# Adapter products in quads, with blocks of up, down, down, up between them, in a TensorE-bound FFN kernel

## The reference, cut to what matters

```python
w = weight[adapter_ids]
y = jnp.einsum('bsi,boi->bso', x, w)              # first products, "lora"
t = y.reshape(b * l, Dm)[:, perm].reshape(b * l, h, d)
t = jnp.einsum('bhd,hdm->bhm', t, up)             # "up"
t = jax.nn.gelu(t, approximate=False)
t = jnp.einsum('bhm,hmd->bhd', t, down)           # "down"
x = x + t.reshape(b * l, h * d)[:, argsort(perm)].reshape(b, l, Dm)
```

## Time and profile before

| | before |
|---|---|
| median of 3 runs | 301.78 us (300.81 to 303.13) |
| profiled execution, its own time | 302.47 us |
| its span (first to last instruction) | 300.6 us |
| mean granted TensorE clock | 0.997 |
| PE busy | 293.7 us, 98% of the span |
| DVE busy | 177.6 us, 59% |
| ACT busy | 159.0 us, 53% |
| POOL busy | 98.7 us, 33% |

### The profile page before, as it was taken

How to read it: one execution, slowest core, us unless ns; L and a number is a source line. 1 busy time by engine, 2 the same in 40 slices (tenths; PEclk the granted TensorE clock), 3 DMA queues, 4 the chain that set the end, 5 groups by cost and what they waited for, 6 DMA issues and landing times.

```text
span 300.6 us, 4303 instructions
## 1 busy us (share of the span) xinstructions
PE 293.7 (98%) x1672; PEld 211.3 (70%) x1672; DVE 177.6 (59%) x210; ACT 159.0 (53%) x179; POOL 98.7 (33%) x92
## 2 busy tenths in 40 slices
PE   8999999999999999999999999999999999999994
PEld 3778888888888758586685857858587685544441
DVE  2778769769765963594736847466564723333332
ACT  3637336347439462854429363392824507777750
POOL 3000000188250064181632617130471535222234
PEclk9999999999999999999999999999999999999998
DMA  6999999999996878579675767755376193421335
GB/s 201 324 426 422 420 419 409 317 338 394 393 365 231 340 269 324 177 247 324 221 293 209 277 237 267 271 195 190 120 253 222 70 303 120 136 73 70 139 142 209
DMA packets 23555, 77.87 MB, mean 259 GB/s; under 512 B 2672, under 2 KB 11248, under 8 KB 18544
## 3 DMA queue, kind: packets, MB, share of 16 engines
q1 hardware_dynamic: 6912, 43.39, 39.2%
q0 software_dynamic: 7488, 25.18, 23.4%
q10 hardware_dynamic: 9136, 9.05, 8.8%
HBM read 60.82 MB, written 16.78 MB: 258 GB/s over the span
## 4 chain that ended last, share of the span: by engine, by line
PE 91%; DMA 3%; SPq 2%; issue 1%; DVE 1%; POOL 1%; ACT 0%; POOLq 0%; DVEq 0%
PE ps L535 38%; PE ps L536 19%; PE ps L584 18%; PE ps L563 6%; PE ps L566 5%; PE ps L569 5%; DMA w_raw<-w 3%; SPq L217 1%; POOL out_late L286 1%; SPq L194 1%; DVE w_lo L405 0%; ACT w_hi L317 0%; DVE w_raw L438 0%; SPq L223 0%; POOLq L307 0%
## 5 line engine op out<-in xcount | busy, mean ns | idle before, releaser
L535 PE MATMUL ps<-x_pair,w_hi 128*128 128x512 f32 x480 | 171.0, 401 | 0.7 <-DVE w_lo L405 0.7
L536 PE MATMUL ps<-x_pair,w_lo 128*128 128x256 f32 x480 | 134.7, 281 | 0.0
L535 PEld LDWEIGHTS ps<-x_pair,w_hi 128*128 128x128 f32 x480 | 90.2, 188 | 29.9 <-issue 7.2
L351 ACT ACTIVATE hidden<-ps 128x1024 f32<-128x1024 f32 x64 | 61.0, 1030 | 63.3 <-PE ps L569 56.6
L317 ACT ACTIVATE w_hi<-w_raw 128x1024 fp32r<-128x1024 f32 x60 | 60.4, 1060 | 60.4 <-PE ps L536 32.3
L536 PEld LDWEIGHTS ps<-x_pair,w_lo 128*128 128x128 f32 x480 | 90.6, 189 | 0.0
L405 DVE TENSOR_TENSOR w_lo<-w_raw,w_hi 128x1024 fp32r<-128x1024 f32 x60 | 70.7, 1219 | 13.6 <-ACT w_hi L317 13.6
L259 POOL DMA_INDIRECT t_raw<-y_rows,idx x32 | 33.6, 1049 | 107.7 <-DMA y_rows<-y_out 86.1
L429 DVE TENSOR_REDUCE y_out<-ps 128x256 f32<-128x512 f32 x64 | 42.6, 686 | 41.1 <-PE ps L536 28.5
L584 PE MATMUL ps<-hidden,down_sb 128*64 128x512 f32 x256 | 58.2, 598 | 0.0
L584 PEld LDWEIGHTS ps<-hidden,down_sb 128*64 128x64 f32 x256 | 17.0, 136 | 33.4 <-issue 33.0
(11 more groups left out here) (28 smaller groups left out, 112.5 us busy)
## 6 DMA issues: line engine op xcount, KB each, us to landing
w_raw<-w SPq DMA_DIRECT2D x30, 1024.0 KB
y_rows<-y_out ACTq DMA_DIRECT2D x32, 256.0 KB
x_raw<-x_cols SPq DMA_DIRECT2D x7, 1024.0 KB, 8.0
w_raw<-w SPq DMA_DIRECT2D x4, 256.0 KB, 4.8
hidden<-up SPq DMA_DIRECT2D x1, 1024.0 KB, 10.0
down_sb<-down SPq DMA_DIRECT2D x1, 1024.0 KB, 9.8
w_raw<-w SPq DMA_DIRECT2D x2, 384.0 KB, 7.1
x_raw<-x_cols ACTq DMA_DIRECT2D x2, 256.0 KB, 3.6
```

The lines of the kernel that those rows point to most:

```text
L351: nc.scalar.activation(hidden[:, f % HS, m, :, :], up_banks(f, m)[:, :, :], ACT.Gelu).then_inc(gelu_done, 1)
L535: nc.tensor.matmul(acc, w_hi[:, ws, k, col], x_pair[:, xs, k, :, :], start=(k == 0), stop=False)
L536: last = nc.tensor.matmul(acc[:, 0, :], w_lo[:, ws, k, col], x_hi[:, xs, k, :], start=False, stop=(k == KT - 1))
```

## The change

The lora units go by quads q (one batch each). Behind quad 2 comes up pair 0 alone; behind each of the quads 3 to 6 a block of four pairs, for block k = q - 2: up pair 2k - 1, down pair 2k - 2, down pair 2k - 1, up pair 2k. Nothing stands behind quad 7 but the rest: up pair 9, down pair 8, up pair 10, and so on in turn. The banks and the waits on them follow from the new order, and ACT, DVE and POOL get orders of their own to match. `w_high` of the unit after the next now stands ahead of `y_park` of the same unit, except the one for unit 4q + 5, which stands behind the quad, ahead of the gelus of up pair 2k. Warm-up matmuls write `ps[3]` in place of `ps[0]`.

The core of the diff, PE's order and its waits first:

```diff
-            for j in range(GROUPS):
-                if j > 0:
-                    for g in lora_of(j):
+            for q in range(QUADS):
+                k = block_behind(q)
+                for g in lora_of(q):
+                    if g >= PAIR:
                         lora_unit(g)
-                for f in up_of(j):
+                if k:
+                    for f in units(2 * k - 1):
+                        up_unit(f)
+                    for f in units(2 * k - 2):
+                        down_unit(f)
+                    for f in units(2 * k - 1):
+                        down_unit(f)
+                if k is not None:
+                    for f in units(2 * k):
+                        up_unit(f)
+            for p in range(TURNS, PAIRS):
+                for f in units(p):
                     up_unit(f)
-                for f in down_of(j):
+                for f in units(p - 1):
                     down_unit(f)
+            for f in units(PAIRS - 1):
+                down_unit(f)
```

```diff
 # lora_unit
-                j = g // PAIR
-                if g >= 2 * PAIR:
-                    pe.wait_ge(y_summed, OT * PAIR * (j - 1))
-                if j == LEAD + 1:
-                    pe.wait_ge(gelu_done, g % PAIR + 1)
-                elif g % PAIR == 0 and up_of(j - 1):
-                    pe.wait_ge(gelu_done, MT * (up_of(j - 1)[0] + 1))
-                if g % PAIR == 1 and down_of(j - 1):
-                    pe.wait_ge(added, down_of(j - 1)[-1] + 1)
+                q = g // QUAD
+                if q > LEAD:
+                    f = PAIR * 2 * (q - LEAD - 1) + g % QUAD // 2
+                    pe.wait_ge(gelu_done, MT * f + g % 2 + 1)
+                elif q > 0:
+                    pe.wait_ge(y_summed, OT * (g - 1 if g % QUAD < 2 else g - 5))
 # up_unit
+                behind_quad = p == 0 or p % 2 == 1 and p <= TURNS
+                q = (p + 1) // 2 + LEAD
                 if f == 0:
-                    pe.wait_ge(up_lo_done, len(UP_GROUPS))
-                    pe.wait_ge(y_summed, OT * PAIR * j)
+                    pe.wait_ge(up_lo_done, len(UP_UNITS))
+                if behind_quad:
+                    pe.wait_ge(y_summed, OT * (QUAD * q + (4 if p == 0 else 2 * (f % 2 + 1))))
+                elif f % 2 == 1:
+                    pe.wait_ge(added, f - 1 if p < TURNS else f - 3)
 # down_unit, new for each half m
+                    pe.wait_ge(gelu_done, MT * f + m + 1)
```

```diff
 # ACT
+            for q in range(QUADS):
+                k = block_behind(q)
+                for g in lora_of(q):
+                    if q >= LEAD and g % QUAD == (0 if q > LEAD else QUAD - 1):
+                        for f in units(2 * (q - LEAD) - 1 if q > LEAD else 0):
+                            t_high(f)
+                    if g % QUAD == (0 if q > LEAD else 2) and q + 1 < B:
+                        x_high(q + 1)
+                    if g % QUAD < 3 and g + 2 < NL:
+                        w_high(g + 2)
+                    y_park(g)
+                    if q == UP_QUAD and g % QUAD in UP_UNITS:
+                        up_high(UP_UNITS.index(g % QUAD))
+                if k:
+                    for f in units(2 * k - 1):
+                        gelu(f)
+                        t_high(f + PAIR)
+                if QUAD * q + 5 < NL:
+                    w_high(QUAD * q + 5)
+                if k is not None:
+                    for f in units(2 * k):
+                        gelu(f)
 # DVE
+            for q in range(QUADS):
+                k = block_behind(q)
+                for g in lora_of(q):
+                    if q >= LEAD and g % QUAD == (0 if q > LEAD else QUAD - 1):
+                        for f in units(2 * (q - LEAD) - 1 if q > LEAD else 0):
+                            t_low(f)
+                    if g % QUAD == (0 if q > LEAD else 2) and q + 1 < B:
+                        x_low(q + 1)
+                    y_sum(g)
+                    if g % QUAD < 3 and g + 2 < NL:
+                        w_low(g + 2)
+                    if q == UP_QUAD and g % QUAD in UP_UNITS:
+                        up_low(UP_UNITS.index(g % QUAD))
+                if k:
+                    for i in range(PAIR):
+                        t_low(PAIR * 2 * k + i)
+                        add_x(PAIR * (2 * k - 2) + i)
+                    for f in units(2 * k - 1):
+                        add_x(f)
+                if QUAD * q + 5 < NL:
+                    w_low(QUAD * q + 5)
 # POOL
+            gather_t_pair(0)
+            for f in range(3):
+                gather_rows(f)
+            gather_t_pair(1)
+            gather_t_pair(2)
+            for k in range(BLOCKS):
+                if k > 0:
+                    gather_t_pair(2 * k + 2)
+                    scatter_pair(2 * k - 2)
+                gather_t_pair(2 * k + 3)
+                if k > 0:
+                    scatter_pair(2 * k - 1)
+                pool.wait_ge(lora_done, OT * (QUAD * (k + LEAD + 1) + 1))
+                for f in range(4 * k + 3, 4 * k + 7):
+                    if f < LATE:
+                        gather_rows(f)
+                for b in LATE_BLOCKS.get(k, ()):
+                    gather_late_rows(b)
```

More of the change, by code:

```diff
@@ L45 @@
 YS, TG, SS, HS, XR = 4, 6, 2, 4, 9
-PAIR, LEAD = 2, 6
-L_GROUPS = NL // PAIR
+PAIR, QUAD, LEAD = 2, 4, 2
+QUADS = NL // QUAD
 PAIRS = NF // PAIR
-GROUPS = PAIRS + LEAD + 1
-UP_GROUPS = (4, 5)
-UP_HEADS = FU // len(UP_GROUPS)
+BLOCKS = QUADS - LEAD - 1
+TURNS = 2 * BLOCKS - 1
+UP_QUAD, UP_UNITS = 2, (0, 2)
+UP_HEADS = FU // len(UP_UNITS)
 UP_AFTER, DOWN_AFTER = 7, 9
 LATE = NF // 2
-LATE_BLOCKS = {7: (0, 1), 8: (2, 3), 9: (4, 5, 6, 7)}
+LATE_BLOCKS = {3: (0, 1), 4: (2, 3, 4, 5, 6, 7)}
 SPLIT_BLOCKS = (FU - 2, FU - 1)
@@ L159, in row_place, with lora_of, block_behind, up_set @@
             return late_rows[:, f % FU, late_half(f)] if f >= LATE else rows[:, f % XR, :]
[L161 to L168, removed]
+        def lora_of(q):
+            return range(QUAD * q, QUAD * (q + 1)) if q < QUADS else range(0)
+        def block_behind(q):
+            return q - LEAD if 0 <= q - LEAD < BLOCKS else None
+        def up_set(f):
+            p = f // PAIR
+            if p < TURNS:
+                return ((p + 1) // 2 + 1 - p % 2 + f) % 2
+            return (p - TURNS + BLOCKS + f) % 2
+        def units(p):
+            return range(PAIR * p, PAIR * (p + 1)) if 0 <= p < PAIRS else range(0)
         def up_banks(f, m):
-            j = f // PAIR + LEAD
-            return ps[2 * ((j + f) % 2) + m]
+            return ps[2 * up_set(f) + m]
         def down_bank(f):
-            j = f // PAIR + LEAD + 1
-            return ps[2 * (j % 2)][:, f % 2, :]
+            p = f // PAIR
+            if p < TURNS - 1:
+                return ps[2 * ((p // 2 + 1) % 2) + p % 2][:, f % 2, :]
+            return ps[2 * ((p + 1 - TURNS + BLOCKS) % 2)][:, f % 2, :]
         def y_bank(g, o):
-            j = g // PAIR
[L180 to L185, removed]
+            return ps[2 * ((g // QUAD + g % QUAD // 2) % 2) + g % 2][:, o, :].rearrange("p (c s) -> p c s", c=2)
         def w_landed(g):
@@ L378, in _ @@
             first_w_high(1, PIECES - 1)
-            for j in range(GROUPS):
-                if j < L_GROUPS:
-                    if PAIR * j % LPB == PAIR and PAIR * j // LPB + 1 < B:
-                        x_high(PAIR * j // LPB + 1)
-                    for f in up_of(j):
[L385 to L392, removed]
+            for q in range(QUADS):
[21 more added lines that the diff above has]
+            for p in range(TURNS, PAIRS):
+                for f in units(p):
                     gelu(f)
-                    if split_ahead(j):
+                    if p + 1 < PAIRS:
                         t_high(f + PAIR)
-                if j + 1 < L_GROUPS:
-                    w_high(PAIR * (j + 1) + 1)
         @block.vector
@@ L461, in _ @@
             first_w_low(1, PIECES - 1)
-            for j in range(GROUPS):
-                if j > 0:
-                    for f in down_of(j - 1):
-                        add_x(f)
[L467 to L472, removed]
-                        t_low(f)
[L474 to L487, removed]
+            for q in range(QUADS):
[16 more added lines that the diff above has]
+                    for f in units(2 * k - 1):
+                        add_x(f)
+                if QUAD * q + 5 < NL:
+                    w_low(QUAD * q + 5)
+            for p in range(TURNS, PAIRS):
+                if p + 1 < PAIRS:
+                    for f in units(p + 1):
+                        t_low(f)
+                for f in units(p - 1):
+                    add_x(f)
+            for f in units(PAIRS - 1):
                 add_x(f)
@@ L494, in warm @@
                 for n in range(WARM):
-                    nc.tensor.matmul(ps[0][:, 1, :], ones[:, 0:P], ones, start=True, stop=True)
+                    nc.tensor.matmul(ps[3][:, 1, :], ones[:, 0:P], ones, start=True, stop=True)
```

38 lines of the change are left out of this document (17 added, 21 removed).

## The result

| | before | after |
|---|---|---|
| median | 302.02 us (300.57 to 303.46, 22 runs) | 303.56 us (301.8 to 306.7, 22 runs) |
| profiled execution | 302.47 us, span 300.6 | 302.79 us, span 300.6 |

The ratio is 1.0055, 95% interval 1.0037 to 1.0072 (the run at 306.7 us, counted as slow, is left out of it): the medians lie 1.5 us or half a per cent apart. The forecast was 302.8 us on a base of 301.78, so +1.0. The two spans are equal by chance: the start of the program varies from execution to execution. Before reached lora unit 2 at 19.68 us, after at 18.72 (and at 19.33 to 20.02 in three later profiles of the same kernel). So the stretches are compared, not the spans.

The account below looks back on a forecast made before the run. PE, busy 293.7 of 300.6 us, was taken as the bound, so only its stream's length and holes count. Terms -1.4 - 0.2 + 2.6 = +1.0 us on 301.78 gave 302.8 us, range 300.2 to 305.4.

Parts of the forecast that it names:

- Part 1: PE's stream: fewer entries into and exits from lora, and down pairs joined in one stretch, save 1.4 us.
- Part 2: ACT: w_high ahead of y_park closes the hole at lora unit 4, 0 to -0.2 us, taken as -0.2.
- Rival D: Changes of product cost what they did, since the delay belongs to the waits there: 304.2 us, chance 0.08.
- Part 3: First block: up unit 0 waits for unit 11's sum, lora unit 12 for gelu(0): a loss of 2.6 us.
- Rival A: DVE and ACT reach the first block in time, 1.3 us or less lost: 301.5 or 300.2 us, chance 0.17.
- Part 4: Blocks behind quads 3 to 6: every wait has named cover, so they cost 0.
- The smallest cover: Up pair 2k's second unit waits for down pair 2k - 1's last add, there 0.6 us ahead of need.
- rival B: In each block the second up unit waits for a late last add: 306.8 us; with other late steps, chance 0.12.
- The cover in quad 3: Behind the late first block, the next quad's cover on ACT and DVE shrinks to about 1 us but stays.
- rival C: Clock drops to 1.2 GHz behind the first block's hole, doubling the up pair: +3.0 us, 305.8 us, chance 0.05.

Follow-up runs that it names:

- E7: E4 with x_high(4) and x_low(4) put back to the middle of quad 3: 300.77 us, ratio 0.9966 to before.
- E5: Before with one move alone, w_high(3) ahead of y_park(1) on ACT: 302.09 us, ratio 1.0008 to before.
- E1: After with the banks of quads 0 to 2 exchanged, so up unit 0 need not wait for unit 11's sum: 303.41 us, ratio 1.0051 to before.
- E2: After with w_high(13) behind the four gelus of up pair 0 on ACT: 303.97 us, ratio 1.0065 to before.
- E3: After with the edits of E1 and E2 together: 302.23 us, ratio 1.0007 to before.
- E4: E3 with x_high(3) and x_low(3) one lora unit earlier: 301.54 us, ratio 0.9985 to before.
- E9: After unchanged, run again for its profile: 303.11 us at a mean clock of 1.0.
- E11: After unchanged, run again for its profile: 304.90 us at a mean clock of 0.992.
- E8: Before with up unit 0 waiting for the sum of lora unit 13, delayed by idle DVE reductions: 305.05 us, ratio 1.0116 to before.
- E6: After with two idle DVE reductions ahead of up_low(1), results unused: 306.91 us, ratio 1.0156 to before.
- E10: After unchanged, run again for its profile: 304.94 us at a mean clock of 0.992.

## Why the prediction was right, point by point

**Part 1, fewer changes of product: right.** -1.4 us was the sum, -1.6 with part 2. Two down pairs take 7.0 us where 7.16 stood before, four lora units 22.8 us where twice 11.49 stood. E7, with 0.2 us of the first block left, gains 1.4 us from lora unit 2 on; after loses 0.9 there with 2.6 in the first block, which leaves a gain of 1.7. Rival D (no gain) falls.

**Part 2, w_high ahead of the park: right,** -0.2 us, in the profiles of after and of E5.

**Part 3, the first block: right, by its mechanism and to 0.1 us.** Forecast: DVE's sum ends 2.1 to 2.2 us too late; measured, a hole of 2.10. Forecast with the gelu behind the copy: 2.6 us in all; measured 2.6 by the starts, of which the two holes are 2.46. That the gelu's chain alone sets the total is what E1 shows. The profile gives "issue" and not the gelu as what released lora unit 12; that it is the gelu, E2 shows, where the hole goes with the earlier gelu. Not seen: t_low(0) would be late on its own (0.34 us in E1), though the sum of part 3 has it: its steps put the start of the two t_low at 76.06, so the first ends near 76.7, behind the 76.47 at which up unit 0 should start. Rival A falls: the slack of ACT and DVE in the mean helped nothing here.

**Part 4, the blocks: right** for the kernel as it is, no hole in any of them, so rival B falls. The smallest cover was forecast at 0.6 us and is that: in the first block the last add ends at 113.97 + 0.69 = 114.66 by DVE's timeline of after, and the second up unit, half a pair behind 113.78, starts at about 115.3. The cover in quad 3, named as 1 us, was real: E3 and E4 spent it and lost 0.8 us.

**The clock, rival C: undersized as a chance, oversized as a price.** I gave it 0.05 and +3.0 us. It comes in half of the executions (13 of 25, with E9 to E11) and costs 1.1 us in two profiles. So one of the prediction's own signs of being wrong, a granted clock under 1.00 behind the first block, came true in half of the executions; the sum has no term for it. Part of rival C is therefore right beside the forecast, and the range was wide enough to hold both.

How much of the median that explains is an estimate. The move was +1.5 us where +1.0 was forecast; another 0.24 of the distance from 302.8 to 303.56 is only the base, 301.78 in the three runs of the forecast and 302.02 in the 22. Half of 1.1 us on +1.0 makes +1.55, which would close the account. But within after's 22 runs the low executions have a median of 304.94 and the others of 302.47 us, 2.5 apart and not 1.1 (in E1, E2 and E8 the two kinds lie 1.7, 1.3 and 1.2 apart), and the others lie only 0.45 above before (0.8 by the means). The good fit of the median may thus be in part luck; what the rest between the two kinds is stays open.

The Trainium skill ("TensorE: Matmul & The Clock Gate", Part 1) says that an idle PE falls back to half rate and needs sustained work to regain it; the rows of E6, E10 and E11 agree, with 0.50 granted in or behind the hole and 1.00 again after 4 to 5 us of work.

## What to carry to other kernels

Where one engine is 98% busy, count first what the new order saves on it, then walk the other engines' queues up to the first place where the new order makes it wait: one block of a kind of its own (here the first, with extra work from up_low and t_low in front of it) can take more than all the regular blocks give. A wait that starts a chain must be cleared together with the chain; either edit alone (E1, E2) gained nothing that the medians show, both with two moves of x gained 0.9% on the changed kernel and 0.3% on the old one. Ask also what the repair pushes back in its turn, as it did w_low(14) in E3 and E4. A hole in TensorE's stream can cost more than its length: here 1.1 us more for one of 2.1 us, when the clock fell behind it.

## What the runs showed of the hardware that I had not expected

With holes of 2.1 to 2.25 us in an otherwise dense stream the granted clock was lowered in about half of the executions (after 13 of 25, E2 7 of 12, E8 3 of 6); one of 4.3 us lowered it in all of 6; E1, with its 2.4 us split into 0.3, 0.2 and 1.8, in 2 of 12; E3, E4, E5 and E7, with holes under 1 us, in none of 48. These are small counts of different kernels, so they show that longer holes bring it more often, and no exact chance. A mean clock of 0.992 in place of 0.998 looks like nothing, and was the sign of a low stretch behind such a hole in both profiles that had it. The small rest that before shows, 0.997 in its profile, lies behind the last matmuls: 1.00 up to 296.3 us, 0.80 from there to 300.6.
